# Record stage of a graph network kernel: ranks, feature product, order of the TensorE products and of the evictions

## The reference

```python
ea = jax.nn.silu(edge_attr @ We + be)      # edge_attr_16 (E, 16), We (16, 128)
Eh = (edge_attr @ WE).reshape(-1, H, dh)   # edge_attr_128 (E, 128), WE (128, 128)
temporal_encodings = temporal_features @ T_w.T + T_b   # edge_attr_64
agg = jax.ops.segment_sum(x[src], dst, num_segments=N)
```

## Time and profile before

| | us |
|---|---|
| median of 3 runs | 15174.92 |
| lowest and highest | 15158.39, 15202.58 |
| the profiled execution | 15231.38 |
| its span (first to last instruction) | 15229.6 |

### The profile page before, as it was taken

How to read it: one execution, slowest core, us unless ns; L and a number is a source line. 1 busy time by engine, 2 the same in 40 slices (tenths; PEclk the granted TensorE clock), 3 DMA queues, 4 the chain that set the end, 5 groups by cost and what they waited for, 6 DMA issues and landing times.

```text
span 15229.6 us, 238216 instructions
## 1 busy us (share of the span) xinstructions
PE 10563.9 (69%) x62195; PEld 9046.0 (59%) x62196; DVE 6470.2 (42%) x15380; ACT 4068.9 (27%) x8630; POOL 4671.6 (31%) x4705
## 2 busy tenths in 40 slices
PE   4999999903767767677368876677777776455554
PEld 3666666603666656666357865566666665455553
DVE  3222222201453544535524537546446457444445
ACT  0111111101213041230421133332432433344443
POOL 1222222260240604316003304214124034355553
PEclk7555555557989989898688998897887888777886
DMA  8222222289645646465198568668578477333334
GB/s 281 84 84 83 83 84 84 81 20 101 201 136 214 175 158 191 142 209 157 39 273 247 163 216 259 195 223 246 181 232 246 171 239 222 87 107 105 109 107 73
DMA packets 2304037, 2401.06 MB, mean 158 GB/s; under 512 B 693528, under 2 KB 1723623, under 8 KB 2303515
## 3 DMA queue, kind: packets, MB, share of 16 engines
q1 hardware_dynamic: 1981702, 1411.29, 33.0%
q0 software_dynamic: 301504, 974.53, 21.5%
q10 hardware_dynamic: 20693, 13.65, 0.3%
HBM read 1477.74 MB, written 921.21 MB: 158 GB/s over the span
## 4 chain that ended last, share of the span: by engine, by line
PE 47%; DMA 13%; issue 12%; DVE 9%; ACT 7%; SPq 6%; another core or an unknown queue 5%; DVEq 2%; ACTq 1%; POOL 0%; POOLq 0%
PE ps L797 16%; DMA row_b<-node_row_s 11%; PE ps L781 6%; PE ps L761 4%; PE ps L762 4%; PE ps L740 3%; PE ps L752 3%; PE ps L745 2%; DVE gath L1380 2%; ACT gath L1012 2%; PE ps L818 2%; SPq L581 2%; PE ps L801 2%; ACT gath L1005 2%
## 5 line engine op out<-in xcount | busy, mean ns | idle before, releaser
L781 PE MATMUL ps<-big,onehot 125*128 x19584 | 2932.4, 298 | 1543.2 <-DVE onehot L1356 1368.8
L672 POOL DMA_INDIRECT gath<-msg_units,unit_at_d x2176 | 2238.4, 1029 | 5740.4 <-DMA msg_units<-gath 4125.9
L781 PEld LDWEIGHTS ps<-big,onehot 125*128 125x128 f32 x19584 | 2511.5, 202 | 1965.6 <-issue 1960.4
L797 PE MATMUL ps<-onehot,gath 128*128 128x125 f32 x17408 | 2820.9, 323 | 1139.1 <-ACT gath L1012 590.9
L797 PEld LDWEIGHTS ps<-onehot,gath 128*128 128x128 f32 x17408 | 2535.6, 229 | 1424.4 <-issue 577.7
L1356 DVE TENSOR_SCALAR onehot<-row_b,part 125x512 f32<-125x512 uint8 x2448 | 1190.6, 486 | 3088.0 <-DMA row_b<-node_row_s 2436.9
L1005 ACT ACTIVATE gath<-ps 128x512 f32<-128x512 f32 x2176 | 1299.2, 597 | 2583.8 <-PE ps L781 2583.8
L1373 DVE TENSOR_TENSOR onehot<-iota,node_d 128x500 f32<-128x500 f32 x2176 | 1466.2, 674 | 257.3 <-issue 233.6
L682 POOL DMA_INDIRECT big<-kv_table,src_at x1088 | 1064.8, 979 | 1124.6 <-DVE gath L1458 619.1
L646 POOL DMA_INDIRECT rec<-big,idx_ring x832 | 797.6, 959 | 1956.2 <-ACT big L992 1725.1
L1387 DVE TENSOR_TENSOR big<-big,ps 128x125 f32 x2448 | 693.5, 283 | 1289.8 <-PE ps L797 1055.0
(11 more groups left out here) (213 smaller groups left out, 11909.1 us busy)
## 6 DMA issues: line engine op xcount, KB each, us to landing
msg_units<-gath SPq DMA_DIRECT2D x2176, 256.0 KB, 3.9
big<-rec SPq DMA_DIRECT2D x1360, 256.0 KB
row_b<-node_row_s SPq DMA_DIRECT2D x2176, 62.5 KB
att_units<-big SPq DMA_DIRECT2D x273, 388.0 KB, 5.0
big<-in_attr_t SPq DMA_DIRECT2D x208, 256.0 KB
rec<-big SPq DMA_DIRECT2D x1, 42640.0 KB, 150.2
big<-rec SPq DMA_DIRECT2D x272, 132.0 KB, 4.8
gath<-msg_units,unit_at_d POOLq DMA_INDIRECT x2176
```

The lines of the kernel that those rows point to most:

```text
L672: pool.indirect_dma_start(ring[:, q, :, :].rearrange("p k f -> p (k f)"), None, units, bass.IndirectOffsetOnAxis(ap=unit_at[w][:, g:g + 1] ...
L781: ins = pe.matmul(ps[:, r, c], onehot[0:NT, r, c], big[0:NT, ds(at_[q] + NA * NODES_PAD, D)], start=True, stop=True)
L797: ins = pe.matmul(ps[:, RING + r, 0:NT], ring[:, q, j, 0:D], hots[:, r, j, :], start=j == 0, stop=j == UNIT - 1)
```

## The change

- **Keys.** The keys go to DRAM once, as 16 bit integers, instead of twice as floats (once negated). SP loads them as one broadcast: each of 128 partitions gets the group's 512 keys. VectorE compares this row with the edge's own key (a column of `bucket`) in the ranking instruction itself. The four difference products on TensorE, the semaphore `diffs` and the use of PSUM bank 1 for them are gone; bank 1 becomes the second buffer of the turned one-hots.
- **16 wide features.** Instead of four products over 17 partitions, one product over 68: the four columns' features stand under each other as stationary operand, and the moving one, `a16_w`, 512 wide, holds `ea_w` four times along a block diagonal. SP loads it in four pieces per group in place of one.
- **Order on TensorE.** A group's transposes now stand at the end of the group before it. Each add to the table is followed by one 128 wide feature product, so that this stands between an add and the next one. The look-up follows, and then the one 68 row product.
- **Order on ScalarE.** Four copies of the table, the copy of the next group's turned one-hots, and then the evictions of the group before.
- **One-hots** are made two groups ahead and have four buffers. SP's loads wait for `rec_mm` in place of `rec_ready`.

The core of the diff (`...` marks what is left out; the other edits are the buffers' shapes and the semaphore counts):

```diff
@@ SP, scatter
+                for k in range(PER):
+                    sp.dma_start(a16_w[k * (A16 + 1):(k + 1) * (A16 + 1), k, :], A["ea_w"]).then_inc(loaded, 16)
...
                         if not first:
-                            sp.wait_ge(rec_ready, RING * i + q - RING + 1)
                             sp.wait_ge(ranked, RING * i + q - RING + 1)
+                            sp.wait_ge(rec_mm, RING * i + q - RING + 1)
                         cols = ds((i * RING + q) * PER * P, PER * P)
-                        sp.dma_start(key_a[0:1, q, :], key_row[0:1, cols]).then_inc(key_in[q], 16)
-                        sp.dma_start(key_b[1:2, q, :], key_row[1:2, cols]).then_inc(key_in[q], 16)
+                        sp.dma_start(key_b[:, q, :], key_row[cols].partition_broadcast(P)).then_inc(key_in[q], 16)
                         sp.dma_start(attr_t[:, q, :], A["attr128_t"][:, cols]).then_inc(att_in[q], 16)
-                        sp.dma_start(a16_t[:, q, :], A["attr16_t"][:, cols]).then_inc(att_in[q], 16)
+                        for k in range(PER):
+                            sp.dma_start(a16_t[k * (A16 + 1):(k + 1) * (A16 + 1), q, :],
+                                         A["attr16_t"][:, ds(((i * RING + q) * PER + k) * P, P)]).then_inc(att_in[q], 16)
@@ PE, scatter
+                def turn(g, q, first):
+                    pe.wait_ge(pair_hot, g + 1)
+                    if not first:
+                        pe.wait_ge(kept, g - 1)
...
+                    for k in range(PER):
+                        last = pe.transpose(ps[0:BKT, q % 2, k * P:(k + 1) * P], oh_e[:, q, 0, k, :], ident[:, :])
+                    last.then_inc(turned, 1)
+
+                def lap(i, first, last_lap):
                     for q in range(RING):
                         g, r = RING * i + q, q % 2
...
+                        if not (last_lap and q == RING - 1):
+                            turn(g + 1, (q + 1) % RING, first and q == 0)
+                        pe.wait_ge(att_in[q], 16 * (1 + PER) * (i + 1))
+                        if not first or q >= 2:
+                            pe.wait_ge(rec_ready, g - 1)
                         for k in range(PER):
                             c = slice(k * P, (k + 1) * P)
-                            last = pe.matmul(ps[:, 1, c], key_a[:, q, c], key_b[:, q, c], start=True, stop=True)
-                        last.then_inc(diffs, 1)
-
-                        for k in range(PER):
                             pe.wait_ge(tab_kept, PER * g + k + 1)
...
                                       skip_group_check=True).then_inc(run_ready, 1)
+                            pe.matmul(ps[:, 4 + r, c], attr_t[:, q, c], weight("we"), start=True, stop=True)
...
-                        pe.wait_ge(att_in[q], 32 * i + 32)
-                        if not first or q >= 2:
-                            pe.wait_ge(rec_ready, g - 1)
-                        for k in range(PER):
-                            c = slice(k * P, (k + 1) * P)
-                            pe.matmul(ps[:, 4 + r, c], attr_t[:, q, c], weight("we"), start=True, stop=True)
-                            last = pe.matmul(ps[:, 6 + r, c], a16_t[:, q, c], ea_w[:, :], start=True, stop=True)
-                        last.then_inc(rec_mm, 1)
+                        pe.matmul(ps[:, 6 + r, :], a16_t[:, q, :], a16_w.rearrange("p k d -> p (k d)"), start=True, stop=True)\
+                          .then_inc(rec_mm, 1)
@@ ACT, scatter
+                def trip(i, head, last):
...
+                        if not (last and q == RING - 1):
+                            keep(g + 1, (q + 1) % RING, head == 0 and q == 0)
+
+                        if q:
+                            evict(g - 1, q - 1, None if head == 0 else i)
+                        elif head != 0:
+                            evict(g - 1, RING - 1, None if head == 1 else i - 1)
@@ DVE, scatter
-                        dve.wait_ge(diffs, g + 1)
+                        dve.wait_ge(key_in[q], 16 * (i + 1))
                         for k in range(PER):
-                            last = dve.scalar_tensor_tensor(same[:, k, :], ps[:, 1, k * P:(k + 1) * P], 0.0, lower, ALU.is_equal,
+                            last = dve.scalar_tensor_tensor(same[:, k, :], key_b[:, q, k * P:(k + 1) * P],
+                                                            bucket[:, ds(g * PER + k, 1)], lower, ALU.is_equal,
                                                             ALU.mult, accum_out=rank_e[:, k:k + 1])
```

114 lines of the change are left out of this document (56 added, 58 removed).

## The result

| | kernel before | changed kernel |
| --- | --- | --- |
| median of the runs, us | 15,168.83 (4 runs, 15,158.39 to 15,202.58) | 14,365.26 (4 runs, 14,328.39 to 14,380.46) |
| ratio, 95% interval | | 0.946 (0.944 to 0.949) |
| profiled execution, us (span) | 15,231.38 (15,229.6) | 14,380.46 (14,378.7) |
| mean granted clock over the span | 0.774 | 0.785 |

The change makes the kernel 5.4% faster. I had forecast 13,520 us with a range from 13,440 to 13,880, so the direction was right and the time was missed by 845 us: half of the forecast gain came.

A forecast was written before the change was run, and what follows sets the result against it. It took TensorE at the low clock to bound the record stage, expected the clock to rise and GpSimd to set 5.2 us: 208 x (13.24 - 5.2) = 1,672 us saved, 13,520 us forecast, range 13,440 to 13,880.

The forecast's parts named there:

- What bounds the kernel: Record stage: TensorE's own sequence, 93% busy at clock 0.50, 13.24 us per group, 208 groups, 18% of the span.
- I expect the rise in the first groups, and then no fall.: Record stage: the new order's nearly gapless stream, some 6 of 8.2 us, lifts TensorE's clock from 0.50 to 1.00.
- Feature products, 4 x 0.47 = 1.9: TensorE, low clock: four 128-row feature products per group take 1.9 us in place of their half of 5.79.
- the sum as written, 8.5: TensorE's group at the low clock: transposes 1.0, features 1.9, adds 1.7, wide product 1.9, look-up 2.0; taken as 8.2 us.
- Rival 1: Record stage: the clock stays low, the group is TensorE's 8.2 us, time 14,130 us; chance 15%.
- Difference products, 2.00: TensorE, each group: removing the four difference products takes away 2.00 us.
- cost nothing: ScalarE's later evictions cost nothing, as four PSUM banks for two groups are free long before TensorE comes round.
- Product of 68 rows, 1.9 at the low clock: TensorE: one 512-column product without reloads takes at most 1.9 us, about 1.8 by gapless instructions.
- GpSimd next at 5.1 to 5.3 us: Record stage: GpSimd's four indirect issues per group, 1.27 us each, become the next bound; 5.2 us taken.
- TensorE at the high clock, 5.1: A group on TensorE at the high clock sums to 5.1 us, perhaps 4.6.
- SP and the buffers' loop, "hidden at 5.2": SP's seven issues take 3.2 us; the loop of 16.5 us over four groups, 4.1 each, stays hidden at 5.2.
- So POOL sets the group: With the clock risen, GpSimd (POOL) sets the record stage's group at 5.1 to 5.3 us, 5.2 taken.

The follow-up runs named there:

- e_adds128: Changed kernel with the dst one-hots 128 wide instead of 51, table and turned copy in 128 rows, zeros behind the 51; 14,210 us.
- e_all128: Changed kernel with dst one-hots, look-up table and the wide 68-row product all filled up to 128 by zeros; 14,132 us.
- e_before_pad: Kernel before with only the 17-row feature operands laid in 128 rows, the others zero; 14,579 us, ratio 0.956.
- e_wide128_one: Changed kernel with the 68-row product filled up to 128 rows by zeros and one load of attribute rows per group instead of four; 12,889 us, ratio 0.890.
- e_wide128_again: Changed kernel with the 68-row product filled up to 128 rows by zeros, four attribute loads kept, run again in set 3; 13,027 us.
- e_one_load: Changed kernel with one load of attribute rows per group in place of four, nothing else; 14,416 us, ratio 0.946.
- e_wide128: Changed kernel with only the 68-row product filled up to 128 rows by zeros, four attribute loads kept, set 1; 14,116 us.
- e_wide128_one_third: e_wide128_one run a third time, unchanged, in set 4 beside a kernel before at 15,236 us; 14,173 us, ratio 0.930.
- e_no_alt: Changed kernel with the four 128-row feature products in a row behind the look-up instead of one behind each add; 13,478 us, ratio 0.930.

## Why the prediction was wrong, point by point

- **What bounds the kernel.** Right: TensorE's row of products, at clock 0.50. All of the gain is in the record stage, 208 groups, and the other stages kept their length.
- **"I expect the rise in the first groups, and then no fall."** This is the step that failed: the clock stayed at 0.50 for all of the stage, and the group at TensorE's 9.10 us instead of GpSimd's 5.2. How much of the miss of 845 us it carries depends on the chip. On the other kind the risen clock and the single load give 795 us (13,677 to 12,882). On the kind that I forecast for, the risen clock gives 243 us, and the other 600 are a second step, told in the last point of this list. The evidence that I used, and the earlier trace rows, was true but read for the wrong property: the stretches in which the clock rose were not only gapless, they used 125 or 128 rows in every product. I counted the product of 68 rows among those "at one height or nearly". e_adds128 (99.4% busy, 0.50) against e_all128 (75% busy, 0.79), which differ in the rows of one product and where its operand lies, separates the two. e_before_pad shows it in the kernel before, with the operand where it was. The earlier trace rows already held the warning that I named, 93% busy at 0.50; I explained it by the 0.22 gaps of the weight loads, which do not decide it: e_wide128_one has the changed kernel's order and its borders, and keeps 0.98.
- **Feature products, 4 x 0.47 = 1.9.** Mis-sized: 4 x 0.73 = 2.9. The neighbours differ in columns instead of rows, which costs the same. From the sum as written, 8.5: + 1.0 for these, + 0.1 for the wide product (2.00), - 0.3 for the adds (0.34 each instead of 0.42), - 0.15 for the transposes (0.85), so 9.15 against the measured 9.10. The waits for ScalarE's copies between the adds went, as forecast. And from 8.5 I had gone down to 8.2 for fewer changes of height, which the changes of width used up.
- **Rival 1, the clock stays low, 14,130.** This is what happened, given 15%, and it lay 235 us under the measured median mainly for the size of the feature product: 208 x 0.9 = 187; most of the rest is the 56 us that I took off for the profiled execution, which here lies only 15 above the median. The range did not reach to it. The Trainium skill's rule on transposes (page "TensorE: Matmul & The Clock Gate", section "Part 4: PE-mode transpose"), which I had weighed for this rival, does not tell the two cases apart: e_adds128 and e_all128 transpose alike, and the first stays at 0.50 while the second has 0.79. Whether transposes count, no run here shows.
- **Difference products, 2.00.** Right as a term of the sum, but not by itself: taken out alone they give 1.2 (13.24 to 12.0), since TensorE then waits for ScalarE's evictions. I had said that the later evictions "cost nothing" and not that they earn anything; they are worth 0.58.
- **Product of 68 rows, 1.9 at the low clock.** 2.00 measured, right within 5%, but credited with the wrong merit: four 17-row products in a row also take 2.00, and the transposes behind them 0.17 more.
- **GpSimd next at 5.1 to 5.3 us.** Right as a bound, out of reach for the changed kernel: e_wide128_one runs at 5.13 to 5.26 with GpSimd's issues 1.26 to 1.36 us apart. Its 0.890 of the kernel before is also my forecast's ratio (13,520 / 15,175 = 0.891), but on the other kind of chip.
- **TensorE at the high clock, 5.1.** Right by luck, since its parts cancel: in e_wide128_one the adds and feature products take 2.6 instead of 2.2 (4 x 0.65), and the transposes, the look-up and the wide product 2.55 (0.44, 1.06, 1.05) instead of 2.95. A feature product takes 0.42 there, not 0.29.
- **SP and the buffers' loop, "hidden at 5.2".** Nearly: four loads instead of one cost 0.7 us per group once TensorE is fast (e_wide128_again against its neighbour), nothing at 9.1 (e_one_load).
- **"So POOL sets the group", at a risen clock.** This is the second step that fails on this kind of chip: there a group takes 7.9 to 8.1 us even with the clock at 0.74 to 0.79 (e_wide128, e_all128, e_wide128_one_third), 2.9 us over 5.2, which is 600 us in 208 groups. What these stretches are is open. They were not foreseeable from the record stage before, which has none, but waits for "remote" of 12.75 and 8.62 us stand in the view that the rows from 13306.24 us in the earlier trace rows are taken from, and I passed over them. So even with the clock risen the changed kernel would have come out near 0.93 of the kernel before on this kind of chip, about 14,100 us, and outside my range.

## What to carry to other kernels

When a stage sits at the low clock although TensorE is busy, look at how many rows its products use before looking for gaps: zeros up to 128 rows cost the products nothing here and brought the clock up in all three kernels that were filled up in the group's feature products (the changed one, e_adds128 and the one before). Keep products of the same size (rows, weight columns) next to each other; each product with a border of sizes ahead of it cost 0.16 to 0.3 us more at the low clock, so that filling waits with products of another size can cost about as much as the waits (9.00 us without it in e_no_alt at the low clock, 9.10 with it). And before a step is counted as pure gain, ask what it had covered: the difference products hid ScalarE's evictions, and about half of their price came back until those were moved. Last, a bound at a faster clock is only as good as the stretches that nobody explains: look through the other stages for waits with no cause before you count on it.

## What the runs showed of the hardware

- The granted clock followed the rows in use in these kernels. 100% busy with products of 51, 68 and 128 rows: 0.50 over 1800 us. The same stream with the 68-row product filled up to 128 by zeros: 0.75, on the other kind of chip 0.89, and 0.98 with the single load. The kernel before with 17-row products filled up: 0.61 instead of 0.50. Multiplying by zeros counted. In e_adds128 the look-up had 128 rows and the clock stayed at 0.50; the rows of the 512-column product made the difference to e_all128. In e_no_alt no row was added, only the 128-row products stood together, and the clock averaged 0.59: the order counts too, and rows alone are not the whole rule, which stays open.
- A 128-by-128 product (two passes) took 0.43 us beside its like and 0.72 to 0.73 beside a product of 17 rows or of 51 columns, at the low clock; a look-up of eight passes 1.96 with 51 rows between other sizes and 1.67 with 128 rows (e_adds128). At the high clock an add and a feature product took 0.23 and 0.42.
- The same kernel ran at 14,492 to 14,496 us on two chips and at 15,169 to 15,236 on the others. The longer ones have stretches of 5 to 12 us in which ScalarE, VectorE and TensorE wait for nothing that the profile shows, while GpSimd goes on issuing. In the record stage they show in none of the kernels that take 8.3 us and more per group (the changed kernel has the same stage on both kinds), and cost 2.9 us per group where 5.2 would be possible. What they are stays open.
